# First attention of a four-layer kernel: the clamp of the exponentials moves from Pool to VectorE, the normalisation of x from VectorE to Pool

## The reference

```
def _layernorm(x, axis=-1, eps=1e-05):
    m = jnp.mean(x, axis=axis, keepdims=True)
    v = jnp.var(x, axis=axis, keepdims=True)
    return (x - m) / jnp.sqrt(v + eps)
...
    # L0_attn_a: B, T, D = 8, 256, 256; H = 16 heads of 16; h is the layer norm of x
    Q = Q * cos + _rotate_half(Q) * sin
    K = K * cos + _rotate_half(K) * sin
    scores = jnp.einsum('bhqd,bhkd->bhqk', Q, K) / np.sqrt(hd).astype(np.float32)
    scores = jnp.where(cam[None, None, None, :], scores, neg)     # 153 of 256 keys stay
    probs = jax.nn.softmax(scores, axis=-1)
    ...
    out = jnp.einsum('bhqk,bhkd->bhqd', probs, V)
    out = out.transpose(0, 2, 1, 3).reshape(B, T, D) @ wo.T
...
    x = x + _L0_attn_a_ref(_layernorm(x, axis=-1), ...)
    x = x + _L0_ffn_ref(_layernorm(x, axis=-1), ...)
    x = x + _L0_attn_b_ref(_layernorm(x, axis=-1), ...)
    x = x + _L0_ffn_ref(_layernorm(x, axis=-1), ...)
```

## Time and profile before

| | |
|---|---|
| median of 3 runs | 940.77 us (940.66 to 945.98) |
| the profiled execution's own time | 944.91 us |
| its span, first to last instruction | 942.9 us |
| mean granted TensorE clock | 0.971 |
| PE busy | 856.5 us, 91% of the span |
| DVE busy | 717.7 us, 76% |
| ACT busy | 531.3 us, 56% |
| POOL busy | 434.7 us, 46% |

### The profile page before, as it was taken

One profiled execution on the slowest core, in us unless ns is written; L12 is line 12 of the kernel. 1 busy time (PEld: TensorE's weight loads), 2 busy tenths in 40 slices (PEclk: granted clock), 3 DMA queues, 4 the chain that ended last, 5 costly groups with the idle time before them and its releaser, 6 DMA issues.

```text
span 942.9 us, 19230 instructions
## 1 busy us (share of the span) xinstructions
PE 856.5 (91%) x6286; PEld 649.1 (69%) x6286; DVE 717.7 (76%) x2366; ACT 531.3 (56%) x1392; POOL 434.7 (46%) x683
## 2 busy tenths in 40 slices
PE   6678898889999999987999999999999997999996
PEld 5556666667765666655888787887888775666663
DVE  6567988889778887663968787787868686888872
ACT  5356544454354555545676676757586761555555
POOL 0348898887766665446202121221202012556655
PEclk9779999999999999989999999999999999999999
DMA  6333333332223557102112020202021022234331
GB/s 211 60 50 49 53 56 55 56 55 38 35 37 58 103 118 133 43 14 46 24 24 46 1 46 1 45 2 46 2 45 37 11 35 35 36 71 59 59 48 35
DMA packets 49938, 46.55 MB, mean 49 GB/s; under 512 B 5280, under 2 KB 47280, under 8 KB 49840
## 3 DMA queue, kind: packets, MB, share of 16 engines
q1 hardware_dynamic: 49840, 45.33, 26.2%
HBM read 11.40 MB, written 2.10 MB: 14 GB/s over the span
## 4 chain that ended last, share of the span: by engine, by line
PE 33%; DVE 15%; issue 3%; ACT 1%; POOL 1%; DMA 0%; POOLq 0%; SPq 0%; DVEq 0%; ACTq 0%
PE bank L301 8%; PE bank L1979 6%; PE bank L1987 4%; PE bank L1913 4%; DVE weights L1476 3%; PE bank L1928 3%; DVE weights L1466 3%; PE bank L1743 2%; PE bank L1756 2%; DVE q_lo L1456 1%; PE bank L1739 1%; DVE rope L1454 1%; PE bank L1782 1%; DVE xn L338 1%; DVE arena L1313 1%
## 5 line engine op out<-in xcount | busy, mean ns | idle before, releaser
L1313 DVE TENSOR_REDUCE arena<-bank 128x2 f32<-128x512 f32 (+1 forms) x192 | 130.9, 685 | 42.4 <-PE bank L1743 41.4
L924 ACT ACTIVATE weights<-bank 128x512 f32<-128x512 f32 x144 | 85.8, 596 | 109.1 <-PE bank L1756 108.3
L1006 ACT ACTIVATE weights<-weights,neg_max 128x128 f32<-128x128 f32 (+1 forms) x256 | 113.9, 449 | 39.2 <-DVE neg_max L1466 38.7
L727 POOL TENSOR_SCALAR_AFFINE_SELECT weights<-weights 128x256 f32<-128x256 f32 x144 | 68.6, 478 | 101.4 <-ACT weights L924 101.4
L1979 PE MATMUL bank<-kbT,arena 128*128 128x128 f32 (+1 forms) x512 | 105.1, 328 | 1.0 <-DVE y L447 0.9
L667 POOL TENSOR_SCALAR weights<-weights 128x512 f32<-128x512 f32 x64 | 97.6, 1537 | 12.5 <-ACT weights L832 12.5
L1743 PE MATMUL bank<-kf_stack,q_stack 96*128 96x256 f32 (+1 forms) x256 | 99.7, 432 | 0.0
L1013 ACT ACTIVATE weights<-bank 128x384 f32<-128x384 f32 x128 | 62.7, 490 | 61.0 <-PE bank L1987 60.5
L1466 DVE CUSTOM_DVE_ANT_0 weights<-bank,arena 128x128 f32<-128x128 f32 (+1 forms) x256 | 80.2, 350 | 14.6 <-PE bank L1979 12.6
L301 PE MATMUL bank<-x_hi,wb_hi 128*128 128x256 f32 x256 | 83.8, 327 | 2.8 <-DVE q_lo L1456 2.8
L1476 DVE TENSOR_SCALAR weights<-weights,inv_sum 128x128 f32<-128x128 f32 (+1 forms) x256 | 81.3, 360 | 4.6
(11 more groups left out here) (236 smaller groups left out, 2514.2 us busy)
## 6 DMA issues: line engine op xcount, KB each, us to landing
q_stack<-q_hi SPq DMA_DIRECT2D x96, 128.0 KB, 4.5
arena<-arena SPq DMA_DIRECT2D x64, 128.0 KB, 2.5
q_stack<-q_lo SPq DMA_DIRECT2D x48, 128.0 KB, 5.3
ka_stack<-k_hi SPq DMA_DIRECT2D x32, 76.5 KB, 2.8
x_all<-x SPq DMA_DIRECT2D x8, 256.0 KB, 5.1
st_wo<-b_wo SPq DMA_DIRECT2D x8, 256.0 KB, 4.2
arena<-b_wqn SPq DMA_DIRECT2D x8, 256.0 KB, 3.3
out<-x_all SPq DMA_DIRECT2D x8, 256.0 KB, 2.1
```

The lines of the kernel that those rows point to most:

```text
L924: a.activation(s["pT"][(STEPS * b + k) % N_PT], p2[k % 2][:, :], ACT.Exp).then_inc(s["exp"], 1)
L1006: last = a.activation(p, p, ACT.Exp, scale=-1.0, bias=neg_max[:, h % 4, t:t + 1], accum_out=sums[:, h % 4, t:t + 1])
L1313: v.tensor_reduce(into, p1[k % 2][:, :].rearrange("p (s g k) -> p s g k", s=n, g=NC), AX.X, ALU.max, negate=True).then_inc(s["maxed"], 1)
```

## The change

`guard` becomes a DVE instruction, at the same steps k, behind the maximum of that step. `dve_normalize` stays on DVE for the first two batches of the first attention and for all other layers; for batches 2 to 7 of the first attention Pool does it, at k=8. Pool's form adds the negated mean and multiplies with `rstd`. For that `pool_rstd` gets one more small instruction, `neg_mean`, in all four layers, and `dve_stats` gets a wait for the normalisation of the batch before it. The wait ahead of the normalisation is now a function, `wait_xn_read`, and says the same as before.

```diff
         def signals(layer, kind, **own):
-            per = dict(stats=4, rstd=2, xn=1, xT=1, x_hi=1, x_lo=1, x_done=1, **own)
+            per = {**dict(stats=4, rstd=3, xn=1, xT=1, x_hi=1, x_lo=1, x_done=1), **own}
...
         def dve_stats(s, b):
             v = nc.vector
+            v.wait_ge(*(at(s, "xn", b, 0) if b or s is sa else at({"f": sa, "b": sf[0], "g": sm}[
+                "g" if s is sf[1] else s["kind"]], "xn", B - 1, 1)))
...
             g.tensor_scalar(var_eps[:, :], mv[:, :, 1], EPS_LN, None, ALU.add).then_inc(s["rstd"], 1)
-            g.wait_ge(*at(s, "rstd", b, 1))
+            g.tensor_scalar(neg_mean[:, :], mv[:, :, 0], -1.0, None, ALU.mult).then_inc(s["rstd"], 1)
+            g.wait_ge(*at(s, "rstd", b, 2))
             g.tensor_tensor(rstd[:, :], var_eps[:, :], expo[:, :], ALU.pow).then_inc(s["rstd"], 1)
...
+        def pool_normalize(s, b):
+            g = nc.gpsimd
+            g.wait_ge(*at(s, "rstd", b, 3))
+            wait_xn_read(g, s, b)
+            for t in range(NT):
+                last = g.tensor_scalar(xn[:, t, :], x_tile(b, t), neg_mean[:, t:t + 1], rstd[:, t:t + 1],
+                                       ALU.add, ALU.mult)
+            last.then_inc(s["xn"], 1)
...
             # Pool's step_a
-                if k == 0 and there(b - 2):
-                    guard(b - 2, 1, G - 1)
-                if k in GUARD_STEPS and there(b - 1):
-                    guard(b - 1, *GUARD_STEPS[k])
+                if k == 8 and b >= 0 and there(b + 2):
+                    pool_normalize(sa, b + 2)
...
             # DVE
+            def guard(b, o, j):
+                dve.wait_ge(*at(sa, "exp", b, o * ITEMS + (j + 2 if j else 1)))
+                p = pT[o * G + j]
+                v.tensor_scalar(p, p, 0.0, None, ALU.max).then_inc(sa["guard"], 1)
...
-                if k == 9 and there(b + 2):
+                if k == 9 and b < 0 and there(b + 2):
                     dve_normalize(sa, b + 2)
...
                 if there(b):
                     maximum_a(b, k)
                     if k % OCT == OCT - 1:
                         clamp(b, k // OCT)
+                if k == 0 and there(b - 2):
+                    guard(b - 2, 1, G - 1)
+                if k in GUARD_STEPS and there(b - 1):
+                    guard(b - 1, *GUARD_STEPS[k])
```

More of the change, by code:

```diff
@@ L93, in hybrid_layers_kernel @@
         rstd = sb("rstd", [P, NT])
+        neg_mean = sb("neg_mean", [P, NT])
         xn = sb("xn", [P, NT, D])
@@ L326, in pool_rstd, with wait_xn_read @@
             g.tensor_scalar(var_eps[:, :], mv[:, :, 1], EPS_LN, None, ALU.add).then_inc(s["rstd"], 1)
-            g.wait_ge(*at(s, "rstd", b, 1))
+            g.tensor_scalar(neg_mean[:, :], mv[:, :, 0], -1.0, None, ALU.mult).then_inc(s["rstd"], 1)
+            g.wait_ge(*at(s, "rstd", b, 2))
             g.tensor_tensor(rstd[:, :], var_eps[:, :], expo[:, :], ALU.pow).then_inc(s["rstd"], 1)
+        def wait_xn_read(eng, s, b):
+            if s is not sa and b == 0:
+                eng.wait_ge(*at(sa if s is sf[0] else sf[0] if s is sm else sm, "xT", B - 1, 1))
+            else:
+                eng.wait_ge(*at(s, "xT", b, 0))
+        def pool_normalize(s, b):
[6 more added lines that the diff above has]
+            last.then_inc(s["xn"], 1)
         def dve_normalize(s, b):
             v = nc.vector
[L332 to L336, removed]
+            v.wait_ge(*at(s, "rstd", b, 3))
+            wait_xn_read(v, s, b)
             for t in range(NT):
@@ L660, in x_lo_a @@
                 g.tensor_tensor(x_lo[:, :, :], hT, x_hi[:, :, :].bitcast(f32), ALU.subtract).then_inc(sa["x_lo"], 1)
[L662 to L667, removed]
             def step_a(b, k):
```

## The result

The changed kernel takes 946.38 us (17 runs, 944.66 to 948.29), the kernel before beside it 942.43 us (17 runs): ratio 1.0041, 95% interval 1.0029 to 1.0053. It is 0.4% slower, where -3 us had been forecast. The profiled execution took 945.30 us for a span of 943.6.

What follows compares the result with a forecast made beforehand. A ring of waits among nearly full PE, DVE and Pool in the first attention was taken as the bound. Batch steps 1 to 5 at -4 us plus 1 us in 6 to 8 gave -3 us: 937.8 us, range 929 to 950.

Steps and rivals of the forecast that it cites:

- Pool's guard at step 6 is on the ring: First attention: Pool's guard ahead of `var_eps` delays the loop of waits; moving it frees 1.45 us a batch.
- the ring: First attention: PE, DVE and Pool, almost equally loaded, hold one another in a loop of waits, 27.10 us a batch.
- The batch steps 1 to 5, 0.8 us each, -4 us: First attention, where guards and normalisation both move: L643 ends 0.8 us earlier a batch, 4 us gained in all.
- covered: DVE from step 9 to 14 of a batch, where it waits: three added guards (steps 8, 11, 13) cost nothing.
- bound: DVE from step 14 to step 8 of the next batch step, hardly waiting: five added guards cost 2.05 us.
- I leave 1 us exposed, between 0 and 6: Batch steps 6 to 8: 25 guards add 10 us on DVE with no normalisation removed; 1 us lengthens the run.
- In the other layers nobody waits for it: `neg_mean` on Pool, 0.3 us with its gap between statistics and `rstd`, costs nothing outside the first attention.
- (a): Rival: DVE becomes the bound, +5 us in batch steps 1 to 5, some +4 in 6 to 8; 950 us, chance 0.18.
- (b): Rival: Pool's normalisation is late at 1.49 us per instruction, gain shrinks to 0.1 us a batch; 941.3 us, chance 0.2.
- (c): Rival: DVE and PE lose most waits for one another, up to 2.2 us a batch; -11, 930 us, chance 0.15.

## Why the prediction was wrong

- **"Pool's guard at step 6 is on the ring": right.** Moved alone it gains 6 to 7 us from step 7 of batch step 4 to step 15 of 5, and every kernel without it on Pool has that gain. Moving all 40 early guards gains 7.4 us, hardly more than this one.
- **The batch steps 1 to 5, 0.8 us each, -4 us: right in the sum, and that in part by luck.** With late guards on Pool the change gives -4.6 us (0.9951), without `neg_mean` -6.3 us. But it is not 0.8 us a batch: from the clamp at step 15 of batch step 0 on, batch steps 1 to 3 take 83.1 us in the changed kernel against 82.3 before, and 4 and 5 take 49.7 against 54.4. The prices were right (guard 0.419 us against 0.406 to 0.444 forecast; normalisation 0.68 us at the median, 1.62 us for the pair against 1.7; `xn` at 153.91 us, 0.67 us ahead of the transposes, which waited for ACT), and so were "covered" (1.6 us for 24) and "bound" (0.42 us each). The list of DVE's waits in the covered part was short by one, 1.03 us for PE at 158.30 us, which makes that part only more covered.
- **"I leave 1 us exposed, between 0 and 6": this term failed, and set the sign.** The late guards cost 8.5 us with `neg_mean` (0.9951 to 1.0041) and 6.2 without. The reason given was that DVE waits only 5.6 us for PE in 75 us, so that PE holds the layer. Where the guards were added it does not: in these 15 us of the kernel before DVE is busy 14.24 us and PE 12.79.

```profile
190.00:205.00 15.00, 12.79 (x115) 9.40 (x114) 14.24 (x43) 6.63 (x16) 10.90 (x12) 1.00 0.14 34
```

- **What the term left out** is a normalisation that takes 2.57 us when Pool's two-input instructions run beside it, as in the earlier trace rows. In batch step 6 it stays on DVE, as it belongs to the next layer. The forecast had counted on the rotation starting earlier once the guard at step 6 is gone from Pool; here that same shift puts L657 and L663 beside the pair instead of one short instruction (2.57 us against 1.63). The guards of steps 5 and 6 put off what stands behind them on DVE by 0.33 and 0.74 us and the pair by another 0.94: 2.0 us, by which PE's wait grows from 0.75 to 2.75 us, and then comes a slower clock. By the clamp of 6, k=7 that makes 2.3 us (15.8 against 13.5) of the 7.7 that the table has in the end (111.6 against 103.9). The rest comes behind it: at the clamp of 7, k=7 PE waits 1.79 us in the changed kernel and 0.32 in the one before. No run took that part by itself.
- **"In the other layers nobody waits for it", 0.3 us a batch: mis-sized.** `neg_mean` costs 4 us in the changed kernel (1.0041 to 0.9999), and 4.8 us in the kernel before. Its length was right (0.22 us); what it sets off in batch step 2 was not in the sum. In the changed kernel the first table has some 1.5 us of it at 5, k=15 and at 6, k=7, and 4 at 7, k=15; what brings it on there stays open.
- **The clock was no term at all.** The earlier trace rows gives 0.93 for its stretch, so it was on show that it falls. The forecast asked neither after what it falls nor what a longer wait of PE would bring on.
- **The rivals.** (a), DVE becomes the bound, had the right engine and sign, from the wrong place: its 5 us in batch steps 1 to 5 did not come, and in 6 to 8 more came than its 4 us (from 188 to 270 us PE's weight loads wait 6.7 us for maxima, 3.3 before). (b) fell with the 0.68 us. (c) is what batch steps 4 and 5 show, 25.0 us for the batch above, under the bound of 25.5 set for it; it did not last. The sum that was measured: -4.6 + 8.5 = +3.9 us, both terms with `neg_mean`.

The Trainium skill (SBUF — State Buffer, section "Who interferes with whom") has it that of VectorE and GpSimd, which share a port pair, whoever issues first gets it for the whole instruction and the other fully blocks. The rows of the changed kernel agree for two-input instructions of Pool: at 151.22 us a guard on DVE behind the L663 of 151.02 took 1.36 us, against a median of 0.42. They do not for one-input ones: `guard_first` at 152.50 us took 0.41 us while Pool's L349 ran, from 152.29 to 153.91.

```profile
151.22 1.36 DVE L1144 TENSOR_SCALAR weights<-weights 128x512 f32<-128x512 f32 x1
152.50 0.41 DVE L1150 TENSOR_SCALAR arena<-arena 128x512 f32<-128x512 f32 x1
```

## What to carry over

Where a change spans several stages, sum it stage by stage, and ask for the part that only adds work (here the last three batches, where nothing was taken from DVE) what long instruction stands right behind it, and what the emptied engine will run beside it; a part that only adds should be left out of the change first. Few waits of an engine in a long stretch do not say that another one holds it where work is added; its busy time over the short stretch does. A total that does not move can hide a gain and a loss: compare the traces stage by stage before calling a step idle. In a ring of three nearly full engines the smallest instruction ahead of the longest chain is worth a run of its own.

## What was not expected of the hardware

- One instruction of 0.22 us on Pool, once a batch, made the program 4.8 us longer; its trace has a wait of PE of 1.18 instead of 0.93 us, followed by 6 us at a granted clock of 0.72.
- A guard of 1.5 us on Pool had kept Pool's two-input rotation from running beside DVE's normalisation: the pair took 1.63 us with it, 2.12 without any guards, and 2.57 with the guard on DVE.
- Leaving out 64 guards of 1.5 us on Pool gained 17 us, and 64 of 0.42 us on DVE 18 us: by time on the engine 95 against 27 us.
- Pool's form with two per-partition operands and two operations on 128x256 took 542 ns at least and 684 at the median, under half of the one-operation guard on 128x512 (1485 ns).
